# First attention of a two-layer perceiver: the folded sums of one pair and the turned row of maxima of another written as one step of VectorE's ring of PSUM banks

## The chip, the cores and the metric

The kernel runs on one core of one Trainium2 chip. The metric is the device time of one execution in microseconds; where a kernel is run several times, the median is given. A measurement of this kernel is repeatable to a few tenths of a per cent.

## What is computed

The reference is a stack of small layers over two sequences of 256 tokens of width 256 and two contexts of 4096 tokens of width 192. The change touches only its first layer, a cross-attention with 16 heads of width 16:

```
q = (x @ Wq + bq)    # (2, 256, 256)  -> 16 heads of 16
k = (ctx @ Wk + bk)  # (2, 4096, 256) -> 16 heads of 16
v = (ctx @ Wv + bv)
attn = softmax(einsum('bhqd,bhkd->bhqk', q, k) * 16 ** -0.5)   # 256 x 4096 for each head
x = x + (einsum('bhqk,bhkd->bqhd', attn, v).reshape(B, Nq, Cq) @ Wo + bo)
```

Everything behind it (a low-rank self-attention, an expert layer, a second cross-attention with a long convolution, a retention layer, adapters) is the same in both kernels.

## The kernel before, in words

**Pairs and steps.** The 32 (batch, head) combinations are taken two at a time: NP_ = 16 pairs, p = 0 to 15. Keys and queries lie in SBUF as stacks of 49 rows for each head of the pair, one head in partitions 0 to 48 and the other in partitions 64 to 112, so a matmul of the one and a matmul of the other stand side by side in the array. A pair has 16 steps, j = 0 to 15, each of 256 keys. In step j TensorE (`heads_tensor`) does, in this order:

- `scores(p, j)` (line 817, matmuls of line 827): keys by queries, transposed, 256 keys of both heads, four matmuls of 256 columns into one of three score banks (4 to 6) for each head. ScalarE takes their exponentials (`exps`, line 906), two ACTIVATEs of 128x512 for each step, into `pT`.
- `ahead(p, j)`: work for the next pair, five steps early (LEAD = 5). As a rule one `max_step` (line 766, matmuls of line 778): the plain scores of 128 queries and 512 keys of both heads, two matmuls of 512 columns. VectorE reduces them to row maxima (line 928, 128x1024 to 128x2). Sixteen such steps make the maxima of a pair.
- `weigh_half` (line 850, matmuls of line 839): the exponentials of earlier steps by V, four matmuls of 256 columns into four strips of 32 partitions of bank 7, recorded as eight since fp32 is done in two passes. The column of ones in V gives the sum of the softmax.

**The ring.** What TensorE makes for VectorE passes through a ring with two places of two banks each: place `at` uses banks 2*(at % 2) and 2*(at % 2)+1. The order of everything that passes is written out in the list `passing`, and `place[...]` gives the index. TensorE raises `max_made` when a place is filled and VectorE raises `max_read` when it has read it; before it fills place `at`, TensorE waits for the read of place `at - 2` (`max_read.at(at - 1)`). VectorE (`heads_vector`) works through `passing` in order. Three things pass besides the max steps:

- **rows** (`turn_rows`, lines 782 to 788; `add_rows`, lines 934 to 938). When the 16 maxima of pair p are there, VectorE reduces them once more to `nmax` (line 931). Two matmuls of 128 columns (line 787) turn them into a row, and VectorE adds that row to the queries `qs` (line 938). `ahead` issues this for pair p+1 in step j = 12 of pair p, right behind the second max step of pair p+2 and ahead of that step's weigh. `scores(p+1, 0)` waits for it.
- **sums** (`add_quarters`, lines 790 to 797; `take_sums`, lines 940 to 943). ScalarE copies bank 7 of pair p-1 to `oT` behind its fourth exponential of pair p (`sum_out`, line 912); `weigh` of pair p waits for that copy. In step j = 4 of pair p, behind the weigh, TensorE adds the four strips with the matrix `fold` (line 795: four matmuls of 128 columns into four strips of 32 partitions, recorded as eight) and VectorE copies the 128x128 result to `sums` (line 943). `sum_out` waits, before it writes `oT` again, until the fold that reads it is done.
- **turned** and the last sums, in pair 15 only: the stored sums are turned and divided by the sums of the softmax (`turn_sums`, `divide_turned`, `add_last`, `divide_last`).

So an ordinary pair fills 18 places: 16 max steps, one rows and one sums. In the steps of pair 14 from j = 11 on there is no next pair left, so no max steps are issued there, only the rows of pair 15.

Of the kernel before, what the change touches and what calls it, by code (L numbers as in the profile page):

```python
# [13 lines left out]
ALU = mybir.AluOpType  # L14
# [3 lines left out]
P = 128  # L18
# [4 lines left out]
S = 256  # L23
# [73 lines left out]
def build(nc, ins, out):  # L97
    pe, act, dve, pool, sp = nc.tensor, nc.scalar, nc.vector, nc.gpsimd, nc.sync
# [4 lines left out]
    def sb(name, shape, dt=F32):  # L103
        size = -(-math.prod(shape[1:]) * BYTES[dt] // 32) * 32
        spot[0] += size
        assert spot[0] <= END, (name, spot[0] - END)
        return nc.alloc_sbuf_tensor_at(name, shape, dt, offset=spot[0] - size)
# [28 lines left out]
    bank = nc.alloc_psum_tensor("bank", [P, 8, 512], F32)  # L136
# [166 lines left out]
    qs = [sb(f"qs{j}", [P, S], F32R) for j in range(3)]  # L303
# [223 lines left out]
    def keys_tensor():  # L527
# [84 lines left out]
    NP_ = NH // 2  # L612
# [11 lines left out]
    sums = sb("sums", [P, NP_ - 1, P])  # L624
    wo, bob = sb("wo", [P, 2, D]), sb("bob", [P, 1, D])
    oT = sb("oT", [P, 2 * S])
    fold = sb("fold", [P, 32])
# [8 lines left out]
    max_made, max_read, nmax_made = (flag(n) for n in ("max_made", "max_read", "nmax_made"))  # L636
    st_made, p_made, pv_made, oT_copied, den_made, o_done = (flag(n) for n in (
        "st_made", "p_made", "pv_made", "oT_copied", "den_made", "o_done"))
# [8 lines left out]
    def ahead(p, j):  # L647
        m, u = p + 1 + (j + LEAD) // 16, (j + LEAD) % 16
        return steps_of(m, u) if m < NP_ else [(NP_ - 1, "rows")] * (m == NP_ and u == 1)

    def beside(p, j):
        out = ahead(p, j) + [(p - 1, "sums")] * (j == 4 and p > 0)
        return out + [(j // TURN1, "turned")] * (p == NP_ - 1 and j in (TURN0, TURN1))

    passing = [what for u in range(16) for what in steps_of(0, u)]
# [5 lines left out]
    place = {what: at for at, what in enumerate(passing)}  # L661
# [103 lines left out]
    def heads_tensor():  # L765
# [16 lines left out]
        def turn_rows(p):  # L782
            at = place[p, "rows"]
            pe.wait_ge(*nmax_made.at(p + 1))
            pe.wait_ge(*max_read.at(at - 1))
            for qt in range(2):
                t = pe.matmul(bank[:, 2 * (at % 2), qt * P:(qt + 1) * P], nmax[:, qt, :], identr[:, :], start=True, stop=True)
            max_made.up(t)

        def add_quarters(p):  # L790
            at = place[p, "sums"]
            pe.wait_ge(*oT_copied.at(p + 1))
            pe.wait_ge(*max_read.at(at - 1))
            for c in range(4):
                t = pe.matmul(bank[32 * c:32 * c + 32, 2 * (at % 2), 0:P], fold[:, :], oT[:, c * P:(c + 1) * P],
                              start=True, stop=True)
            max_made.up(t)

        def add_last():
            at = place[NP_ - 1, "sums"]  # L800
# [78 lines left out]
        for p in range(NP_):  # L879
            for j in range(16):  # L880
                scores(p, j)
                for what in ahead(p, j):
                    pass_on(*what)
                weigh_half(16 * p + j)
                if j == 4 and p:
                    add_quarters(p - 1)
                if p == NP_ - 1:
                    if j in (TURN0, TURN1):
                        turn_sums(j // TURN1)
                    if j == 6:  # L890
                        turn_batch(0)
                    if j == 9:
                        project_batch(0)
# [6 lines left out]
    def heads_scalar():  # L900
        def exps(p, u):
            at = UNITS * p + u
            act.wait_ge(*st_made.at(at + 1))
            if at >= 8:
                act.wait_ge(*pv_made.at(2 * (at // 4 - 2) + 1 + at % 2))
            p_made.up(act.activation(pT[:, at % 8, :], bank[:, 4 + at % 3, :], ACT.Exp))  # L906

        def sum_out(p):
            act.wait_ge(*pv_made.at(16 * (p + 1)))
            if p:  # L910
                act.wait_ge(*max_made.at(place[p - 1, "sums"] + 1))
            oT_copied.up(act.copy(oT[:, :], bank[:, 7, :]))  # L912

        for p in range(NP_):
            for u in range(UNITS):
                exps(p, u)
                if u == 3 and p:
                    sum_out(p - 1)
        sum_out(NP_ - 1)
        act.wait_ge(*turned.at(4))  # L920
        xT_made.up(act.copy(xT[:, :, S:2 * S], bank[:, 1, :].rearrange("p (k n) -> p k n", k=2)))

    def heads_vector():
        def max_step(p, u):
            at, c, qt = place[p, u], u // 2, u % 2
            dve.wait_ge(*max_made.at(at + 1))
            b0 = 2 * (at % 2)
            max_read.up(dve.tensor_reduce(rmax[p % 2][:, :, qt, c], bank[:, b0:b0 + 2, :], AX.X, ALU.max))  # L928
            if u == 15:
                dve.wait_ge(*max_read.at(at + 1))  # L930
                nmax_made.up(dve.tensor_reduce(nmax[:, :, :].rearrange("p t (a m) -> p a t m", a=2)[:, :, :, MAX_ROW],
                                               rmax[p % 2][:, :, :, :], AX.X, ALU.max, negate=True))

        def add_rows(p):
            at = place[p, "rows"]
            rows = slice(0, HALF_P + MAX_ROW + 1)
            dve.wait_ge(*max_made.at(at + 1))
            max_read.up(dve.tensor_tensor(qs[p % 3][rows, :], bank[rows, 2 * (at % 2), 0:S], qs[p % 3][rows, :], ALU.add))

        def take_sums(p):  # L940
            at = place[p, "sums"]
            dve.wait_ge(*max_made.at(at + 1))
            max_read.up(dve.tensor_copy(sums[:, p, :], bank[:, 2 * (at % 2), 0:P]))

        def divide(total, p0, p1, read):
            den_made.up(dve.reciprocal(rden[:, p0:p1, :], total[:, :, :, D0]))
            dve.wait_ge(*den_made.at(den_made.n))
            for qt in range(2):
                t = dve.tensor_tensor(
                    aoc[:, 2 * (p0 // PB) + qt, :].rearrange("p (h a d) -> p h a d", h=PB, a=2)[:, p0 % PB:p0 % PB + p1 - p0],  # L950
                    total[:, :, qt:4:2, 0:D0],
                    rden[:, p0:p1, qt:4:2].rearrange("p h (a d) -> p h a d", d=1).to_broadcast([P, p1 - p0, 2, D0]), ALU.mult)
                if qt == 0:
                    aoc_made.up(t)
                else:
                    read.up(t)

        def divide_turned(b):
            at = place[b, "turned"]
            p0, p1 = b * PB, min((b + 1) * PB, NP_ - 1)  # L960
            if b == 0:
                dve.wait_ge(*powers_made.at(1))
            dve.wait_ge(*max_made.at(at + 1))
            total = bank[:, 2 * (at % 2):2 * (at % 2) + 2, :].rearrange("p b (n c k) -> p (b n) c k", n=4, c=4)
            divide(total[:, 0:p1 - p0], p0, p1, max_read)

        def divide_last():
            at = place[NP_ - 1, "sums"]
            dve.wait_ge(*max_made.at(at + 1))
            divide(bank[:, 2 * (at % 2), 0:P].rearrange("p (n c k) -> p n c k", n=1, c=4), NP_ - 1, NP_, max_read)  # L970

        def add_batch(b):
            if b == 0:
                dve.wait_ge(*turned.at(3))
                xT_made.up(dve.tensor_copy(xT[:, :, 0:S], bank[:, 1, :].rearrange("p (k n) -> p k n", k=2)))
                dve.wait_ge(*x_biased.at(1))
            dve.wait_ge(*proj_made.at(2 * b + 2))
            for i in (2 * b, 2 * b + 1):
                vec.do(dve.tensor_tensor(x[:, i, :], bank[:, 3, i % 2 * D:(i % 2 + 1) * D], x[:, i, :], ALU.add), x_added)

        nmax_zeroed.up(dve.memset(nmax[:, :, :].bitcast(F32), 0.0))
        fold_made.up(dve.tensor_copy(identr[:, :], ident[:, :]))
        pv_zeroed.up(dve.memset(bank[:, 7, :], 0.0))
        for q in range(4):
            fold_made.up(dve.tensor_copy(fold[32 * q:32 * q + 32, :], ident[0:32, 0:32]))
        dve.wait_ge(*nmax_zeroed.at(1))
        for p, u in passing:
            if u == "rows":
                add_rows(p)
            elif u == "turned":  # L990
                divide_turned(p)
            elif u == "sums" and p < NP_ - 1:
                take_sums(p)
                if p == NP_ - 2:
                    add_batch(0)
            elif u == "sums":
                divide_last()
            else:
                max_step(p, u)
        add_batch(1)  # L1000
# [1631 lines left out]
```

## Time and profile before

| | |
|---|---|
| median of 3 runs | 1071.77 us (1068.39 to 1072.86) |
| the profiled execution's own time | 1071.73 us |
| its span in the profile | 1070.5 us |
| PE busy | 927.4 us (87% of the span) |
| DVE busy | 815.2 us (76%) |
| ACT busy | 649.8 us (61%) |
| POOL busy | 303.5 us (28%) |

The span is what the profiler's instruction records cover; the execution's own time has 1.2 us more around it. PE is TensorE's matmuls, PEld its weight loads, DVE VectorE, ACT ScalarE, POOL GpSimd. The loop over the pairs, about 157 to 490 us of the span, is roughly a third of the kernel. In a timeline row the first number is the start in us from the span's beginning and the second the time from the first start to the last end of the merged instructions. The records of consecutive matmuls overlap, since their ends are modelled, so the distance between two starts says more than the length of a record.

### The profile page before, as it was taken

The page shows a single profiled execution, that of the slowest core. Times are in us where ns is not written, and L with a number is a line of the kernel's source. Part 1 is how long each engine was busy: PE and PEld are TensorE (multiplying, and loading weights), DVE is VectorE, ACT ScalarE, POOL GpSimd, SP SyncE. Part 2 cuts the span into 40 slices and gives each one's busy share as a digit, 9 for nine tenths or more (in the row PEclk, how much of TensorE's full clock was granted, in tenths as well). Part 3 has the DMA queues.
Part 4 walks back from the last instruction along what each step waited for, and adds up shares of the span by engine and source line. Part 5 has one row for each costly group of instructions (what it writes and reads, how often), then busy time and mean ns, then how long its engine had stood idle before and what let it go on. Part 6 is the DMA issues. An engine that isn't in the chain of part 4 may idle for free. (4 is left out here: it accounts for less than half of the span.)

```text
span 1070.5 us, 20952 instructions
## 1 busy us (share of the span) xinstructions
PE 927.4 (87%) x7731; PEld 578.0 (54%) x7731; DVE 815.2 (76%) x1703; ACT 649.8 (61%) x1045; POOL 303.5 (28%) x335
## 2 busy tenths in 40 slices
PE   6999669999999999998789996758788778899877
PEld 5989534444444444444466883733455556735545
DVE  5778599999999999961446887998877776269267
ACT  3434307888888888885245435159999999411212
POOL 1000088889800000000121632006454553000021
PEclk9999959999999999999699997666789999898979
DMA  6878933333323333300403308220165225771000
GB/s 203 296 271 281 321 83 76 80 81 77 85 74 84 79 78 83 79 17 1 121 1 103 90 16 219 83 64 1 57 167 149 60 57 156 221 184 59 0 1 20
DMA packets 99320, 111.83 MB, mean 104 GB/s; under 512 B 26658, under 2 KB 75730, under 8 KB 99218
## 3 DMA queue, kind: packets, MB, share of 16 engines
q1 hardware_dynamic: 98738, 110.16, 35.5%
q8 instruction: 62, 1.02, 0.4%
q10 hardware_dynamic: 480, 0.33, 0.1%
q14 instruction: 40, 0.33, 0.1%
HBM read 80.95 MB, written 29.43 MB: 103 GB/s over the span
## 5 line engine op out<-in xcount | busy, mean ns | idle before, releaser
L906 ACT ACTIVATE pT<-bank 128x512 f32<-128x512 f32 x512 | 278.4, 597 | 84.5 <-PE bank L827 66.9
L928 DVE TENSOR_REDUCE rmax<-bank 128x2 f32<-128x1024 f32 x256 | 309.9, 1224 | 19.4 <-PE bank L778 18.4
L839 PE MATMUL bank<-pT,V 128*17 128x256 f32 x2048 | 161.0, 386 | 4.0 <-ACT oT L912 3.9
L1823 PE MATMUL bank<-K1s,qs 97*128 97x512 f32 x256 | 113.3, 546 | 35.1 <-ACT work L1947 14.1
L827 PEld LDWEIGHTS bank<-qs,ks 49*128 49x128 f32 x1024 | 77.7, 186 | 108.2 <-ACT pT L906 97.6
L827 PE MATMUL bank<-qs,ks 49*128 49x256 f32 x1024 | 130.4, 332 | 2.1 <-ACT pT L906 0.5
L778 PE MATMUL bank<-ks,qs 49*128 49x512 f32 x512 | 112.0, 431 | 16.3 <-DVE rmax L928 7.4
L2112 POOL TENSOR_TENSOR total<-total,work 128x1024 f32<-128x1024 f32 x40 | 95.0, 2381 | 32.7 <-ACT work L1947 31.9
L1823 PEld LDWEIGHTS bank<-K1s,qs 97*128 97x128 f32 x256 | 53.4, 220 | 52.2 <-issue 36.1
L2007 DVE MAX8 cand<-work 128x8 f32<-128x128 f32 x384 | 76.4, 282 | 0.0
L839 PEld LDWEIGHTS bank<-pT,V 128*17 128x17 f32 x2048 | 34.4, 95 | 64.5 <-ACT pT L906 44.0
L778 PEld LDWEIGHTS bank<-ks,qs 49*128 49x128 f32 x512 | 51.0, 194 | 28.5 <-DVE rmax L928 15.6
L1857 PE MATMUL bank<-cn,xT 128*128 128x192 f32 x256 | 60.2, 388 | 6.8 <-ACT xT L1957 6.2
L1108 POOL MEMSET mA<- 128x512 f32 x1 | 0.5, 525 | 217.6 <-POOLq L115 217.6
L1857 PEld LDWEIGHTS bank<-cn,xT 128*128 128x128 f32 x256 | 50.7, 227 | 11.7 <-ACT xT L1957 10.4
L1947 ACT ACTIVATE work<-bank,ebias 128x1024 f32<-128x1024 f32 x48 | 53.8, 1127 | 4.5 <-PE bank L1826 4.2
L1826 PE MATMUL bank<-below,minus 128*128 128x512 bf16 x128 | 55.5, 434 | 0.0
L1938 ACT ACTIVATE below<-work,steep_thr,steep 128x2048 bf16<-128x2048 f32 (+1 forms) x26 | 51.7, 1989 | 2.3 <-issue 1.7
L1916 ACT COPY work<-bank 128x1024 f32<-128x1024 f32 x48 | 48.5, 1020 | 0.2 <-PE bank L1823 0.2
L1390 PE MATMUL bank<-xTp,w13p 128*128 128x512 f32 x192 | 47.2, 396 | 0.0
L1048 POOL TENSOR_TENSOR w13p<-w,w13p 128x512 fp32r<-128x512 f32 x16 | 20.5, 1284 | 74.7 <-ACT w13p L1042 74.7
L1390 PEld LDWEIGHTS bank<-xTp,w13p 128*128 128x128 f32 x192 | 35.1, 188 | 7.5
(470 smaller groups left out, 1782.5 us busy)
## 6 DMA issues: line engine op xcount, KB each, us to landing
k_parts_d<-kparts SPq DMA_DIRECT2D x48, 512.0 KB
ks<-k_parts_d SPq DMA_DIRECT2D x384, 64.0 KB, 2.2
K1s<-k_parts_d SPq DMA_DIRECT2D x96, 128.0 KB
cn<-in_ctx SPq DMA_DIRECT2D x32, 384.0 KB, 3.7
cx<-in_ctx SPq DMA_DIRECT2D x16, 384.0 KB, 4.6
w<-in_L_ffn_w SPq DMA_DIRECT2D x32, 128.0 KB, 2.4
w2e<-in_L_ffn_w SPq DMA_DIRECT2D x16, 128.0 KB, 2.4
W<-in_L_xattn_W SPq DMA_DIRECT2D x2, 1024.0 KB, 8.3
```

Of the source, the lines that this page charges most:

```text
L778: t = pe.matmul(bank[:, 2 * (at % 2) + a, :], qs[p % 3][rows, qt * P:(qt + 1) * P], ks[p % 2][rows, c * 512:(c + 1) * 512], start=True, st ...
L827: t = pe.matmul(bank[:, 4 + (at + a) % 3, c * S:(c + 1) * S], ks[p % 2][rows, k0:k0 + P], qs[p % 3][rows, :], start=True, stop=True)
L839: t = pe.matmul(bank[32 * c:32 * c + VW, 7, a * S:(a + 1) * S], V[:, b * NCH + 4 * g + c, h, :], pT[:, (at + 2 * (c // 2) + a) % 8, c % 2 ...
L906: p_made.up(act.activation(pT[:, at % 8, :], bank[:, 4 + at % 3, :], ACT.Exp))
L928: max_read.up(dve.tensor_reduce(rmax[p % 2][:, :, qt, c], bank[:, b0:b0 + 2, :], AX.X, ALU.max))
L1390: t = pe.matmul(bank[:, b0 + k, :], w13p[e % WB][:, wp, k, kt, :], xTp[:, xp, kt, :], start=(n == 0 and kt == 0), stop=(n == 2 and kt == 1))
L1823: m = pe.matmul(bank[:, b0 + c, :], qs1[0:NROW1, b * H1 + h, q], K1s[h][0:NROW1, keys], start=True, stop=(what == "new"))
L1826: m = pe.matmul(bank[:, b0 + c, :], minus[:, :], below[:, keys], start=False, stop=True)
L1857: m = pe.matmul(bank[:, 7, grp % 2 * 256:grp % 2 * 256 + DC], aT[at % 2][:, c, :], cn[at % NCN][:, c, :], start=(n == 0 and c == 0), stop= ...
L1947: s_taken.up(act.activation(home(t)[:, k * 1024:(k + 1) * 1024], bank[:, b0:b0 + 2, :].rearrange("p c n -> p (c n)"), ACT.Exp, bias=ebias[ ...
L2007: m = dve.max(cand[:, g, :], home(t)[:, g * GC:(g + 1) * GC])
L2112: added.up(pool.tensor_tensor(acc[:, part], acc[:, part], home(t)[:, part], ALU.add))
```

## The change

The sums of pairs 0 to 13 have no place of their own any more. The fold of pair p-2 is done in `turn_rows(p)` for p >= 2, behind the two matmuls of the rows, into the second bank of the same place, and `max_made` is raised once, behind the fold. In `add_rows(p)` VectorE adds the row and then copies the folded sums of pair p-2, and raises `max_read` once. In the order of TensorE the fold of pair p-1 moves from step j = 4 of pair p (behind the weigh) to step j = 12 of the same pair (between the rows and the weigh). An ordinary pair fills 17 places then. The sums of pair 14 keep their place in step j = 4 of pair 15, and those of pair 15 theirs at the end. ScalarE's wait in `sum_out` is set to the place that the fold has now.

```diff
     def beside(p, j):
-        out = ahead(p, j) + [(p - 1, "sums")] * (j == 4 and p > 0)
+        out = ahead(p, j) + [(p - 1, "sums")] * (j == 4 and p == NP_ - 1)
...
             for qt in range(2):
                 t = pe.matmul(bank[:, 2 * (at % 2), qt * P:(qt + 1) * P], nmax[:, qt, :], identr[:, :], start=True, stop=True)
+            if p >= 2:
+                pe.wait_ge(*oT_copied.at(p - 1))
+                t = fold_quarters(bank[:, 2 * (at % 2) + 1, 0:P])
             max_made.up(t)
+
+        def fold_quarters(o):
+            for c in range(4):
+                t = pe.matmul(o[32 * c:32 * c + 32, :], fold[:, :], oT[:, c * P:(c + 1) * P], start=True, stop=True)
+            return t
 
         def add_quarters(p):
             at = place[p, "sums"]
             pe.wait_ge(*oT_copied.at(p + 1))
             pe.wait_ge(*max_read.at(at - 1))
-            for c in range(4):
-                t = pe.matmul(bank[32 * c:32 * c + 32, 2 * (at % 2), 0:P], fold[:, :], oT[:, c * P:(c + 1) * P],
-                              start=True, stop=True)
-            max_made.up(t)
+            max_made.up(fold_quarters(bank[:, 2 * (at % 2), 0:P]))
...
-                if j == 4 and p:
+                if j == 4 and p == NP_ - 1:
                     add_quarters(p - 1)
...
             if p:
-                act.wait_ge(*max_made.at(place[p - 1, "sums"] + 1))
+                act.wait_ge(*max_made.at(place[(p + 1, "rows") if p < NP_ - 1 else (p - 1, "sums")] + 1))
             oT_copied.up(act.copy(oT[:, :], bank[:, 7, :]))
...
             dve.wait_ge(*max_made.at(at + 1))
-            max_read.up(dve.tensor_tensor(qs[p % 3][rows, :], bank[rows, 2 * (at % 2), 0:S], qs[p % 3][rows, :], ALU.add))
+            t = dve.tensor_tensor(qs[p % 3][rows, :], bank[rows, 2 * (at % 2), 0:S], qs[p % 3][rows, :], ALU.add)
+            if p >= 2:
+                t = dve.tensor_copy(sums[:, p - 2, :], bank[:, 2 * (at % 2) + 1, 0:P])
+            max_read.up(t)
```

## Rows read from the trace of the kernel before

**Rows 1.** The page: busy tenths in 40 slices of 26.8 us, and the clock.

```profile
PE   6999669999999999998789996758788778899877
...
DVE  5778599999999999961446887998877776269267
ACT  3434307888888888885245435159999999411212
...
PEclk9999959999999999999699997666789999898979
```

**Rows 2.** Windows: busy us (instructions) of PE, PEld, DVE, ACT, POOL; clock, DMA, GB/s.

```profile
160.00:168.00 8.00, 7.89 (x72) 3.43 (x72) 6.51 (x6) 5.61 (x12) 6.71 (x17) 0.74 0.20 51
...
184.00:480.00 296.00, 286.10 (x3253) 131.71 (x3252) 272.14 (x259) 247.06 (x461) 99.50 (x111) 1.00 0.29 75
```

**Rows 3.** Waits of 184 to 480 us: us in total, times, longest.

```profile
ACT pT L906 <- PE bank L827: 33.7, 97, 0.9
DVE rmax L928 <- PE bank L778: 15.1, 41, 0.4
...
PEld bank L778 <- DVE rmax L928: 4.5, 14, 0.3
```

**Rows 4.** Timeline of PE in pair 9, steps 3 to 6.

```profile
354.19 0.51 PE L827 MATMUL bank<-qs,ks 49*128 49x256 f32 x4
...
355.40 0.51 PE L827 MATMUL bank<-qs,ks 49*128 49x256 f32 x4
355.75 0.39 PE L778 MATMUL bank<-ks,qs 49*128 49x512 f32 x2
356.07 0.63 PE L839 MATMUL bank<-pT,V 128*17 128x256 f32 x8
356.51 0.40 PE L795 MATMUL bank<-oT,fold 128*32 128x128 f32 x8
356.85 0.51 PE L827 MATMUL bank<-qs,ks 49*128 49x256 f32 x4
357.46 0.50 PE L778 MATMUL bank<-ks,qs 49*128 49x512 f32 x2
357.89 0.63 PE L839 MATMUL bank<-pT,V 128*17 128x256 f32 x8
358.45 0.50 PE L827 MATMUL bank<-qs,ks 49*128 49x256 f32 x4
```

**Rows 5.** Timeline of DVE over the same steps.

```profile
354.96 2.45 DVE L928 TENSOR_REDUCE rmax<-bank 128x2 f32<-128x1024 f32 x2 [0.36 <-PE bank L778]
357.32 0.28 DVE L943 COPY sums<-bank 128x128 f32<-128x128 f32 x1
358.00 7.37 DVE L928 TENSOR_REDUCE rmax<-bank 128x2 f32<-128x1024 f32 x6 [0.40 <-PE bank L778]
```

**Rows 6.** Fold matmuls of line 795: durations ns min/median/max, first and last start.

```profile
L795 PE MATMUL bank<-oT,fold x120: 272/273/273, 186.1 to 483.9; 128*32 128x128 f32 x120
```

**Rows 7.** Timeline of PE in pair 0, steps 4 and 5, which have no sums.

```profile
164.30 0.50 PE L827 MATMUL bank<-qs,ks 49*128 49x256 f32 x4
...
165.52 0.50 PE L827 MATMUL bank<-qs,ks 49*128 49x256 f32 x4
```

**Rows 8.** Timeline of PE in pair 9, step 12, with the rows.

```profile
366.18 0.40 PE L778 MATMUL bank<-ks,qs 49*128 49x512 f32 x2
366.88 0.41 PE L787 MATMUL bank<-identr,nmax 128*128 128x128 f32 x2 [0.30 <-DVE rmax L928]
367.21 0.63 PE L839 MATMUL bank<-pT,V 128*17 128x256 f32 x8
367.77 0.51 PE L827 MATMUL bank<-qs,ks 49*128 49x256 f32 x4
368.11 0.41 PE L778 MATMUL bank<-ks,qs 49*128 49x512 f32 x2
```

**Rows 9.** Timeline of DVE over step 12 of pair 9.

```profile
367.78 0.41 DVE L938 TENSOR_TENSOR qs<-bank,qs 97x256 fp32r<-97x256 f32 x1
368.56 2.46 DVE L928 TENSOR_REDUCE rmax<-bank 128x2 f32<-128x1024 f32 x2 [0.36 <-PE bank L778]
```

**Rows 10.** Timeline of PE in pair 14, step 12, where no max steps are left.

```profile
472.76 0.44 PE L787 MATMUL bank<-identr,nmax 128*128 128x128 f32 x2
473.13 0.63 PE L839 MATMUL bank<-pT,V 128*17 128x256 f32 x8
473.69 0.51 PE L827 MATMUL bank<-qs,ks 49*128 49x256 f32 x4
```

## The prediction, made before the changed kernel was run

> **What bounds the kernel now.** The page's slices come first, to place the stage that is touched. From about slice 7 to slice 18 PE shows 9 tenths in each slice, DVE 9, ACT 8, and the clock stands at its upper level [rows 1]. This is the loop over the pairs, the only part that the edit reaches. The table of windows says the same of 184 to 480 us: PE 286.1 of 296 us, DVE 272.1, ACT 247.1, with a granted clock of 1.00, that is 2.4 GHz [rows 2]. Three engines lie within 15 per cent of each other, so shares don't decide; the timeline does.
>
> An ordinary step has one pace. In pair 0, which has no sums, steps 4 and 5 start 1.22 us apart (164.30 to 165.52) [rows 7]. VectorE takes six maxima in 7.37 us, 1.23 us for each [rows 5]. Its reduction and TensorE's own sequence (scores, max step, weigh) are equally long, so neither stores a lead over the other: an interruption of TensorE shows at once as an idle VectorE. The list of waits confirms it. TensorE waits for VectorE before a max step 14 times in the window, 4.5 us in all, once for each of the pairs 1 to 14, and VectorE's own idle time is 15.1 us in 41 waits, about three for each pair [rows 3]. So what costs time is the exceptional steps. There are three: the late copy of bank 7 (VectorE idle 0.36 us ahead of step 3's maximum), the sums (idle 0.40 us behind the copy of 0.28 us) [rows 5], and the rows (idle 0.36 us) [rows 9].
>
> **The price of a place for the sums.** In pair 9 the scores of steps 4, 5 and 6 start at 355.40, 356.85 and 358.45: 1.45 and 1.60 us, 3.05 together [rows 4]. Without sums two steps take 2.44 to 2.46. The first part is the fold itself. The second is the ring. VectorE reads the sums in 0.28 us, while the next max step can only be filled once the maximum before has been read: the reduction begun at 356.18 (half of the pair of 2.45 us begun at 354.96) ends at 357.41, and TensorE, ready some 0.35 us behind the scores of 356.85, starts at 357.46 [rows 4, 5]. A short place between two long ones leaves no time to refill. Without it the next max step goes into a place that has been free since 356.19, so the wait is gone and not moved: the scores start at about 356.63 (0.56 us behind the weigh of 356.07, as 357.89 to 358.45), the max step at 356.98, and VectorE goes on at 357.41, where it is done with the one before, instead of 358.00. That is 0.59 us earlier [rows 4, 5]. I take 0.60 us for each pair.
>
> It is removed from pairs 1 to 14. The fold's matmuls are 120 records of 8 each, 15 pairs, 186.1 to 483.9 us [rows 6]; the last of them, in pair 15, stays. So 14 times 0.60 = **8.4 us gained**.
>
> **The price of the fold in the rows' place.** Nothing is dropped: the same four matmuls (eight records of 273 ns that overlap [rows 6]) and the same copy are done in step 12. There TensorE sets the pace. It waits 0.30 us for the place, turns the row at 366.88, weighs at 367.21, scores at 367.77, fills the next place at 368.11, and VectorE starts on it at 368.56 after 0.36 us of idleness [rows 8, 9]. Whatever the fold takes on TensorE delays that chain in full. It can't slip into the wait of 0.30 us, since it stands behind the rows, which wait for the same place.
>
> How long is that? The trace doesn't show a fold between rows and weigh, so there are two bounds. Lower: inserting the fold between weigh and scores moved the scores from 0.56 us behind the weigh to 0.78 us (356.07 to 356.85), so 0.22 us. Upper: from the fold's start to the next start is 0.34 us (356.51 to 356.85) [rows 4]. I take 0.24, near the lower end, because what follows the fold now is a weigh, whose matmuls use strips of 32 columns as the fold's do, and weigh to fold was the quickest handover in these rows: 0.44 us, against 0.56 us from weigh to scores.
>
> The Trainium skill, page "TensorEngine Tiling (Array Packing)", section "Tiling Modes", says that a change of tiling mode drains TensorE. By it the move adds no such change: rows and weigh differ in mode already, and fold and weigh share one. The page would thus put the fold at the lower bound and the time at 1066.5 us, where the upper bound gives 1068.1; the trace agrees as far as the 0.44 against 0.56 us go [rows 4], and no row shows the handover from rows to fold.
>
> A lower end of zero is excluded, as TensorE has no slack in that stretch. 14 times 0.24 = **3.4 us lost** (3.1 to 4.8). In pair 14 step 12 has no max step and VectorE isn't pressed, but there too TensorE is late (0.93 us from rows to scores, 472.76 to 473.69, against 0.89 in pair 9, with no wait between [rows 8, 10]), so I count it in full.
>
> **VectorE's side of the same place.** The copy (0.28 us, some 0.2 of it beyond the end of the operation before [rows 5]) goes behind the add, which ends at 368.19. VectorE then idles until 368.56, later by the fold's 0.24: 0.6 us of cover for 0.28 [rows 9]. I cost it at nothing; without the cover it would be 0.28 us for each pair. The add needs the fold done now. TensorE would finish about 0.24 us behind 367.29, at 367.55 to 367.65, and VectorE is busy with the maximum before until about 367.78 [rows 8, 9]. That hides it too, with only 0.1 to 0.2 us to spare. Late next, if the fold took longer, would be the add and the copy, still within the idle time behind them.
>
> **The moved and changed waits.** TensorE's wait for `oT_copied` in step 12 is for a copy made around step 2 of the same pair, some 12 us earlier: nothing. ScalarE's wait in `sum_out` of the next pair is now for a fold five to six steps back instead of fourteen: nothing; ahead of it stand only exponentials. `scores(p+1, 0)` waits for the read of the rows' place, which ends 0.2 to 0.3 us later, with more than three steps (3.7 us) to spare. The other place of the ring is free by then, so the next max step doesn't wait; the one behind it needs the combined place at about 369.6, over 1 us after the copy. The ring's parity alternates from pair to pair, but 14 places fewer leave pair 15, with its fixed banks, as it was. No DMA is added, removed or passed: SP's and POOL's queues wait on flags of the scores, which only move with the loop.
>
> **The sum.** 8.4 gained less 3.4 lost is 5.0 us. The profiled execution took 1071.73 us, against a median of 1071.77, so I use the median: **1066.8 us**, 0.47 per cent less. By the bounds alone the gain lies between 3.5 and 5.4 us.
>
> **Rivals.**
>
> *The fold is absorbed* (faster than forecast). If TensorE catches up within the steps behind 12, because VectorE's 1.23 us and not TensorE's sequence is the true pace, a part of the 3.4 us comes back. VectorE would then have to find the 0.36 us idle before it elsewhere. For it: both paces agree to 0.01 us. Against it: VectorE's idle of 0.36 us behind the rows isn't recovered today, it simply passes. Time down to 1071.8 - 8.4 = 1063.4, on the way 1065. Chance 0.15.
>
> *The saving is small.* If the fold between two differently shaped neighbours costs 0.34 us, a restart behind it 0.11 (a weigh starts 0.43 us behind the max step that waited, 357.46 to 357.89, and 0.32 behind the one that didn't) and one more slow handover 0.12 (0.56 less 0.44) [rows 4], step 12 gives back 0.57. Then 14 times 0.03 is left, 1071.4. Against it: rows and weigh follow each other within 0.34 us today [rows 8]. Chance 0.15.
>
> *The stall moves along* (slower). The rows' place is longer now, and the next max step may meet it as the sums' neighbour did. Place: TensorE's first max steps behind step 12. Price: fold 0.34, copy 0.28 no longer covered, and the stall of the sums' place, 0.37 us (1.60 less 1.23 [rows 4]), together 0.99. It decides from 0.60 for each pair upward; at 0.99 the loss is 14 times 0.39 = 5.5 us, **1077.3**. Against it: a long place gives TensorE more time to refill, not less. Chance 0.05.
>
> *The change doesn't do what it says* could only be if the sums' stall came from the copy of bank 7. But the stall is at 357.46, and that copy's stands at step 3, in its own idle time [rows 4, 5]. I give it no chance of its own; it falls under the small saving.
>
> **How the numbers follow.** Forecast 0.65, absorbed 0.15, small saving 0.15, slower 0.05. Half a per cent, 5.4 us, is about what a measurement of this kernel can tell from no change, and the forecast lies just inside it. The runs before spread over 1068.39 to 1072.86, so the median itself may be off by 1 to 2 us, and of the forecast's 0.65 about 0.25 comes out faster by over 0.5 per cent. With the absorbed case: faster 0.40, same 0.55, slower 0.05. The range takes in the absorbed case and most of the small saving: 1063.0 to 1071.0.
>
> **What would show it.** In the profile after: scores of steps 4, 5 and 6 of pairs 1 to 14 at 1.22 to 1.23 us (right), or over 1.3 (wrong); no wait of a max step for a maximum in any of these pairs; the distance of step 12's scores to step 13's 2.16 to 2.28 us instead of 1.94 (366.18 less 0.35 to 367.77 [rows 8]); the weigh 0.56 to 0.67 us behind the rows instead of 0.34; copy of the sums straight behind the add, then idle time of 0.3 to 0.4 us. A distance of step 12 over 2.5 would make the forecast wrong, as would a new wait of the scores for the rows, or a stretch at the lower clock within the loop.

## The result and the profile after

The changed kernel takes 1065.32 us (median of 8 runs, 1061.87 to 1069.80), the kernel before 1072.12 (median of 8, 1068.39 to 1072.86). The ratio is 0.9943, with a 95% interval of 0.992 to 0.9965: 0.57 per cent faster, against a forecast of 1066.8 us, 0.47 per cent. The profiled execution of the changed kernel, 1061.87 us, is the fastest of its eight.

The page's head says what did not change: the work. DVE is busy for as long as before, to the tenth of a microsecond, with as many instructions.

```profile
span 1060.6 us, 20938 instructions
...
PE 919.9 (87%) x7731; PEld 573.3 (54%) x7731; DVE 815.2 (77%) x1703; ACT 650.1 (61%) x1045; POOL 303.6 (29%) x335
```

The table of windows shows where the time went. Each row is one stretch, with its length, the busy time of PE, PEld, DVE, ACT and POOL, the granted clock, the DMA share and GB/s. For each kernel the three rows are pair 0, pairs 1 to 14, and what lies behind the last scores of pair 15 (pair 15 itself, 21.4 us up to there in both, is left out). First the kernel before, then the changed one:

```profile
157.31:179.75 22.44, 21.85 (x213) 10.01 (x209) 20.55 (x20) 17.03 (x32) 18.89 (x45) 0.85 0.22 54
179.75:477.33 297.58, 287.47 (x3269) 132.22 (x3267) 276.34 (x262) 248.57 (x463) 103.02 (x120) 1.00 0.30 76
498.74:1070.49 571.75, 466.05 (x3286) 317.65 (x3286) 399.12 (x1216) 313.05 (x427) 155.25 (x106) 0.87 0.30 86
```

```profile
157.25:179.80 22.55, 21.95 (x212) 10.01 (x209) 20.56 (x20) 17.03 (x32) 18.95 (x45) 0.84 0.22 53
179.80:472.35 292.55, 283.91 (x3270) 130.52 (x3268) 276.29 (x262) 248.72 (x463) 103.19 (x120) 1.00 0.30 78
493.77:1060.63 566.86, 461.93 (x3286) 314.57 (x3286) 399.29 (x1216) 313.11 (x427) 155.09 (x106) 0.87 0.31 86
```

Pairs 1 to 14, the only ones that the edit reaches, take 292.55 us instead of 297.58: 5.03 us less, at a clock of 1.00 in both. The other 4.9 us of this pair of profiles lie behind the loop, in code that is the same. More on that below.

Within a pair, the PE timeline of pair 9 shows both terms of the sum. First the scores of steps 3 to 6, then step 12:

```profile
351.39 0.50 PE L832 MATMUL bank<-qs,ks 49*128 49x256 f32 x4
...
352.61 0.51 PE L832 MATMUL bank<-qs,ks 49*128 49x256 f32 x4
...
353.85 0.51 PE L832 MATMUL bank<-qs,ks 49*128 49x256 f32 x4
...
355.08 0.51 PE L832 MATMUL bank<-qs,ks 49*128 49x256 f32 x4
...
362.48 0.51 PE L832 MATMUL bank<-qs,ks 49*128 49x256 f32 x4
362.82 0.40 PE L778 MATMUL bank<-ks,qs 49*128 49x512 f32 x2
363.52 0.41 PE L787 MATMUL bank<-identr,nmax 128*128 128x128 f32 x2 [0.30 <-DVE rmax L933]
363.86 0.43 PE L795 MATMUL bank<-oT,fold 128*32 128x128 f32 x8
364.10 0.61 PE L844 MATMUL bank<-pT,V 128*17 128x256 f32 x8
364.65 0.50 PE L832 MATMUL bank<-qs,ks 49*128 49x256 f32 x4
364.98 0.40 PE L778 MATMUL bank<-ks,qs 49*128 49x512 f32 x2
```

Steps 4 and 5 start at 352.61, 353.85 and 355.08: 1.24 and 1.23 us, where it was 1.45 and 1.60 [rows 4]. The weigh of step 12 stands 0.58 us behind the rows (363.52 to 364.10) instead of 0.34 [rows 8], and step 12 is 2.17 us long (362.48 to 364.65). Over pairs 1 to 13 the mean of steps 4 and 5 together fell from 3.04 to 2.44 us and that of step 12 rose from 1.95 to 2.18. Summed over pairs 1 to 14, steps 4 and 5 gave 8.42 us, step 12 took 3.23, and the other thirteen steps together took 0.15 more, which makes the 5.0 us.

DVE's timeline answers to [rows 5, 9]:

```profile
352.17 9.85 DVE L933 TENSOR_REDUCE rmax<-bank 128x2 f32<-128x1024 f32 x8 [0.35 <-PE bank L778]
...
364.42 0.41 DVE L943 TENSOR_TENSOR qs<-bank,qs 97x256 fp32r<-97x256 f32 x1
364.75 0.28 DVE L945 COPY sums<-bank 128x128 f32<-128x128 f32 x1
365.42 7.39 DVE L933 TENSOR_REDUCE rmax<-bank 128x2 f32<-128x1024 f32 x6 [0.39 <-PE bank L778]
```

Eight maxima follow each other without a break where there were two, the copy, and a gap of 0.40 us. The copy now stands behind the add, and the gap behind it is 0.39 us, about what it was behind the add alone.

The waits of 184 to 480 us have no row any more for a max step that waits for VectorE, which had 14 entries [rows 3]. One wait changed its source: in pair 14, where no maxima are left, VectorE's add now waits 1.5 us for the fold, where it waited 1.1 us for the rows. VectorE's idle time ahead of a maximum is down by a third, from 15.1 us in 41 waits:

```profile
DVE rmax L933 <- PE bank L778: 10.0, 27, 0.4
```

### The profile page after: what moved, and what is told of

The parts are those of the page before. It is cut to its first block and busy times, and to the rows that moved or that the text cites. A ratio compares the mean times of both kernels' runs of the same rounds, so it can differ in the third digit from the quotient of the medians.

```text
span 1060.6 us, 20938 instructions
## 1 busy us (share of the span) xinstructions
PE 919.9 (87%) x7731; PEld 573.3 (54%) x7731; DVE 815.2 (77%) x1703; ACT 650.1 (61%) x1045; POOL 303.6 (29%) x335
## 5 line engine op out<-in xcount | busy, mean ns | idle before, releaser
L1865 PE MATMUL bank<-cn,xT 128*128 128x192 f32 x256 | 56.1, 369 | 6.4 <-ACT xT L1965 6.2
L1834 PE MATMUL bank<-below,minus 128*128 128x512 bf16 x128 | 57.7, 450 | 0.0
L1865 PEld LDWEIGHTS bank<-cn,xT 128*128 128x128 f32 x256 | 47.0, 213 | 11.2 <-ACT xT L1965 10.5
```

Of the source, the lines that this page charges most:

```text
L1834: m = pe.matmul(bank[:, b0 + c, :], minus[:, :], below[:, keys], start=False, stop=True)
L1865: m = pe.matmul(bank[:, 7, grp % 2 * 256:grp % 2 * 256 + DC], aT[at % 2][:, c, :], cn[at % NCN][:, c, :], start=(n == 0 and c == 0), stop= ...
```

## The experiments

Twelve runs followed: seven edited kernels, and five more profiles of the two kernels compared. The table gives, from the profile of each and of the first two, the stretches as above (us), the mean of steps 4 and 5 together and of step 12 over pairs 1 to 13, and the time at the lower clock behind the loop.

| kernel | pair 0 | pairs 1 to 14 | behind the loop | of it at the lower clock | steps 4 + 5 | step 12 |
|---|---|---|---|---|---|---|
| before | 22.4 | 297.58 | 571.8 | 154 | 3.04 | 1.95 |
| before_2 | 23.4 | 297.57 | 572.8 | 167 | 3.04 | 1.95 |
| before_3 | 23.3 | 297.46 | 573.0 | 154 | 3.04 | 1.95 |
| before_4 | 28.0 | 297.39 | 568.9 | 154 | 3.04 | 1.95 |
| changed | 22.6 | 292.55 | 566.9 | 143 | 2.44 | 2.18 |
| after_again | 23.3 | 292.79 | 567.2 | 150 | 2.45 | 2.18 |
| after_3 | 27.9 | 292.55 | 567.3 | 147 | 2.44 | 2.18 |
| no_sums | 27.0 | 289.39 | 568.8 | 150 | 2.44 | 1.95 |
| fold_twice_j4 | 22.4 | 297.41 | 568.0 | 147 | 3.05 | 1.95 |
| fold_twice | 26.1 | 295.52 | 571.7 | 154 | 2.44 | 2.40 |
| own_place | 26.0 | 302.62 | 568.1 | 147 | 2.44 | 2.97 |
| copy_twice | 23.3 | 292.51 | 567.7 | 137 | 2.44 | 2.18 |
| weigh_first | 23.3 | 289.89 | 570.3 | 160 | 2.44 | 1.95 |
| weigh_fold_rows | 27.8 | 288.42 | 567.7 | 143 | 2.45 | 1.82 |

Pairs 1 to 14 repeat within 0.3 us for one kernel, while over the profiles pair 0 moves by 5.6 us and the part behind the loop, whose code no edit touches, by 6.1. So the experiments are read by pairs 1 to 14.

**no_sums.** The gain without the cost.

```diff
-        out = ahead(p, j) + [(p - 1, "sums")] * (j == 4 and p > 0)
+        out = ahead(p, j) + [(p - 1, "sums")] * (j == 4 and p == NP_ - 1)
...
-                if j == 4 and p:
+                if j == 4 and p == NP_ - 1:
                     add_quarters(p - 1)
...
+        sums_filled.up(dve.memset(sums[:, :, :], 1.0))
```

> The kernel before, with the folds and copies of the sums of pairs 0 to 13 left out altogether (the stored sums are filled with ones once, so the attention's output is not the reference's). Theory of the ring: steps 4 and 5 of pairs 1 to 14 take 2.44 to 2.46 us together instead of 3.04, as in the changed kernel, and step 12 takes 1.95 as before. The loop is 8.4 us shorter than before and 3.2 to 3.4 us shorter than in the changed kernel. Rival (what the changed kernel gained in steps 4 and 5 is only its fold's own time on TensorE, 0.22 to 0.34 us for each pair, and the rest comes from somewhere else): steps 4 and 5 at 2.7 to 2.8.

Measured: 8.2 us less than before in pairs 1 to 14 (8.4 in steps 4 and 5, 0.2 back in the other steps), and 3.2 less than the changed kernel. Steps 4 and 5 take 2.44 us. The gain of steps 4 and 5 is the whole place, as the theory has it, and what the changed kernel gives back in step 12 is the rest.

**fold_twice_j4.** Is it the fold's own time, or the place?

```diff
-            for c in range(4):
+            for c in (*range(4), *range(4)):
                 t = pe.matmul(bank[32 * c:32 * c + 32, 2 * (at % 2), 0:P], fold[:, :], oT[:, c * P:(c + 1) * P],
```

> The kernel before, with every fold of step 4 done twice, one behind the other into the same strips. Theory of the ring: TensorE waits for the maximum before in step 5 anyway, 0.27 us behind the point at which it would be ready, and a second fold takes about 0.22 us. So the scores of step 5 come 0.22 us later, the wait shrinks by as much, and steps 4 and 5 together stay at 3.04 to 3.10; the loop grows by 0 to 0.8 us. Rival (the fold's time on TensorE is what the place costs): steps 4 and 5 at 3.26 to 3.38, the loop 3 to 5 us longer.

Its PE timeline, steps 4 and 5 of pair 9:

```profile
354.52 0.51 PE L827 MATMUL bank<-qs,ks 49*128 49x256 f32 x4
...
355.64 0.62 PE L795 MATMUL bank<-oT,fold 128*32 128x128 f32 x16
356.19 0.50 PE L827 MATMUL bank<-qs,ks 49*128 49x256 f32 x4
356.59 0.50 PE L778 MATMUL bank<-ks,qs 49*128 49x512 f32 x2
...
357.58 0.51 PE L827 MATMUL bank<-qs,ks 49*128 49x256 f32 x4
```

Sixteen records where there were eight. Step 4 grows to 1.67 us (354.52 to 356.19) and step 5 shrinks to 1.39 (to 357.58), 3.06 together as before (3.05). Pairs 1 to 14 take 297.41 us, not a tenth more. In step 4 the fold costs nothing: without it TensorE would only stand still for as long, until VectorE has read the maximum before and so the place of the next max step. The rows of before show what is left as the price: that maximum ends at 357.41, the max step starts at 357.46 and VectorE goes on at 358.00 [rows 4, 5]. These 0.59 us pass whatever the fold takes, as long as it fits into the wait, and the copy lies inside them.

**fold_twice.** The same doubling in the changed kernel.

```diff
-                t = fold_quarters(bank[:, 2 * (at % 2) + 1, 0:P])
+                for _ in range(2):
+                    t = fold_quarters(bank[:, 2 * (at % 2) + 1, 0:P])
```

> The changed kernel, with the fold in the rows' place done twice. Theory (TensorE sets the pace in step 12, so the fold is paid in full there): step 12 goes from 2.18 to 2.40 to 2.42 us, the loop grows by 14 times 0.22, 3.1 us. Rival (VectorE sets the pace, or the fold slips into its idle time): step 12 stays within 0.05 us of 2.18, the loop within 0.7 us.

Its PE timeline, in step 12 of pair 9, which runs from 366.82 to 369.21:

```profile
368.21 0.64 PE L796 MATMUL bank<-oT,fold 128*32 128x128 f32 x16
368.67 0.61 PE L845 MATMUL bank<-pT,V 128*17 128x256 f32 x8
369.21 0.50 PE L833 MATMUL bank<-qs,ks 49*128 49x256 f32 x4
```

The weigh starts 0.46 us behind the doubled fold, where it was 0.24. Measured: step 12 at 2.40 us in the mean, pairs 1 to 14 longer by 2.97 us, 0.21 for each. The fold is free in step 4 and paid in full in step 12.

**own_place.** The move without the sharing.

```diff
-        out = ahead(p, j) + [(p - 1, "sums")] * (j == 4 and p > 0)
+        out = ahead(p, j) + [(p - 1, "sums")] * (j == (4 if p == NP_ - 1 else 12) and p > 0)
...
                 for what in ahead(p, j):
                     pass_on(*what)
+                if j == 12 and 0 < p < NP_ - 1:
+                    add_quarters(p - 1)
                 weigh_half(16 * p + j)
-                if j == 4 and p:
+                if j == 4 and p == NP_ - 1:
                     add_quarters(p - 1)
```

> The kernel before, with the sums moved to step 12, right behind the rows and ahead of the weigh, but still in a place of the ring of their own. It has the changed kernel's order of matmuls, without the shared place. Theory of the ring: the fold must wait there until the maximum before the rows has been read, about 0.75 us more than in the changed kernel, and the weigh, the scores and the next max step stand behind it. Step 12 takes 2.9 to 3.1 us, steps 4 and 5 take 2.45; the loop is 9 to 12 us longer than in the changed kernel, that is 4 to 7 us longer than before. Rival (it is the move to step 12 that helps, not the sharing): step 12 at 2.2 to 2.4, the loop within 3 us of the changed kernel.

Its PE timeline in step 12:

```profile
371.84 0.41 PE L787 MATMUL bank<-identr,nmax 128*128 128x128 f32 x2 [0.30 <-DVE rmax L930]
372.97 0.42 PE L795 MATMUL bank<-oT,fold 128*32 128x128 f32 x8 [0.72 <-DVE rmax L930]
373.19 0.64 PE L839 MATMUL bank<-pT,V 128*17 128x256 f32 x8
```

The fold waits 0.72 us for the maximum before the rows. Step 12 takes 2.97 us; pairs 1 to 14 take 302.62 us, 10.1 more than in the changed kernel and 5.0 more than before. Moving alone loses as much as moving and sharing gains.

**copy_twice.** Is VectorE's copy covered?

```diff
-                t = dve.tensor_copy(sums[:, p - 2, :], bank[:, 2 * (at % 2) + 1, 0:P])
+                for k in (p - 1, p - 2):
+                    t = dve.tensor_copy(sums[:, k, :], bank[:, 2 * (at % 2) + 1, 0:P])
```

> The changed kernel, with the copy of the sums in the rows' place done twice (the first into the slot of the next pair, which is overwritten later). Theory (the copy stands in VectorE's idle time behind the add, 0.39 us): a second one takes 0.20 to 0.28 us of it; the idle time falls to 0.1 to 0.2 us, step 12 stays at 2.18 and the loop within 0.5 us. Rival (VectorE sets the pace there): step 12 at 2.38 to 2.46, the loop 2.8 to 3.9 us longer.

Its DVE timeline:

```profile
363.82 0.42 DVE L943 TENSOR_TENSOR qs<-bank,qs 97x256 fp32r<-97x256 f32 x1
364.15 0.48 DVE L946 COPY sums<-bank 128x128 f32<-128x128 f32 x2
364.82 2.46 DVE L933 TENSOR_REDUCE rmax<-bank 128x2 f32<-128x1024 f32 x2 [0.19 <-PE bank L778]
```

The second copy adds 0.20 us, the idle time falls from 0.39 to 0.19, and pairs 1 to 14 stay at 292.51 us. The copy is covered, and the idle time left behind it is almost twice what it adds.

**weigh_first and weigh_fold_rows.** Can the wait of 0.30 us ahead of the rows be filled, and does the order of shapes matter? The first issues the weigh of step 12 ahead of the rows:

```diff
                 for what in ahead(p, j):
-                    pass_on(*what)
+                    if what[1] != "rows":
+                        pass_on(*what)
                 weigh_half(16 * p + j)
+                for what in ahead(p, j):
+                    if what[1] == "rows":
+                        pass_on(*what)
```

> The changed kernel, with the weigh of step 12 issued ahead of the rows and the fold instead of behind them. Theory (TensorE waits 0.30 us for the rows' place and has the weigh to fill that with): the weigh runs during that wait, the rows start at nearly the same point, and the scores of step 13 come 0.3 us earlier. Step 12 takes 1.85 to 1.90 us instead of 2.18, 15 times 0.3 = 4.5 us less than the changed kernel in the loop. Rival (the chain through VectorE, maximum, add, copy, sets step 12): step 12 stays above 2.1 us. Ratio to before 0.988 to 0.993 by the theory, 0.992 to 0.998 by the rival.

The second puts the fold ahead of the two matmuls of the rows as well:

```diff
+            if p >= 2:
+                pe.wait_ge(*oT_copied.at(p - 1))
+                fold_quarters(bank[:, 2 * (at % 2) + 1, 0:P])
             for qt in range(2):
                 t = pe.matmul(bank[:, 2 * (at % 2), qt * P:(qt + 1) * P], nmax[:, qt, :], identr[:, :], start=True, stop=True)
-            if p >= 2:
-                pe.wait_ge(*oT_copied.at(p - 1))
-                t = fold_quarters(bank[:, 2 * (at % 2) + 1, 0:P])
```

> As weigh_first, and the fold ahead of the rows, so that weigh and fold, which both use strips of 32 columns, stand together. Theory: one handover between differently shaped matmuls less, 0.1 us; TensorE could reach step 13 0.4 us earlier than in the changed kernel, and there VectorE (maximum, add, copy without a break) becomes the bound of that stretch at about 0.39. Step 12 takes 1.76 to 1.82 us in pairs 1 to 13, the loop is 5.5 to 6 us shorter than the changed kernel's. Rival (the order of shapes makes no difference): step 12 as in weigh_first within 0.02.

The PE timeline of step 12, weigh_first:

```profile
361.17 0.40 PE L778 MATMUL bank<-ks,qs 49*128 49x512 f32 x2
361.50 0.63 PE L844 MATMUL bank<-pT,V 128*17 128x256 f32 x8
362.05 0.44 PE L787 MATMUL bank<-identr,nmax 128*128 128x128 f32 x2
362.42 0.42 PE L795 MATMUL bank<-oT,fold 128*32 128x128 f32 x8
362.78 0.51 PE L832 MATMUL bank<-qs,ks 49*128 49x256 f32 x4
```

And weigh_fold_rows (line 790 is the rows):

```profile
364.93 0.40 PE L778 MATMUL bank<-ks,qs 49*128 49x512 f32 x2
365.26 0.63 PE L844 MATMUL bank<-pT,V 128*17 128x256 f32 x8
365.70 0.40 PE L795 MATMUL bank<-oT,fold 128*32 128x128 f32 x8
366.04 0.44 PE L790 MATMUL bank<-identr,nmax 128*128 128x128 f32 x2
366.40 0.51 PE L832 MATMUL bank<-qs,ks 49*128 49x256 f32 x4
```

The wait is gone in both. weigh_first gives 2.66 us in pairs 1 to 14, less than the 4.5 of its expectation (which counted pair 0 too): step 12 is 1.95 us, not 1.85 to 1.90. The expectation had the rows start at nearly the same point, but they start 0.88 us behind the max step (361.17 to 362.05) instead of 0.70 (362.82 to 363.52): from weigh to rows are 0.55 us (361.50 to 362.05), against 0.44 from weigh to fold (365.26 to 365.70), and rows to fold and fold to scores, 0.37 and 0.36, are no shorter. In pair 14, where there is no wait to fill, step 12 even grew, from 1.59 to 1.71 us. With the fold beside the weigh step 12 falls to 1.82 us, at the upper end of its expectation, and to 1.57 in pair 14. The 4.13 us less in pairs 1 to 14 stay under the 5.5 to 6 expected of the loop, since step 12 gained 0.36 us in pairs 1 to 13 rather than 0.39, step 13 gave back 0.04 (the next max step comes 0.34 us behind its scores, 366.40 to 366.74, but VectorE's rows show no wait from the add at 366.53 to the maximum at 367.21, so VectorE sets the pace there), and step 12 of pair 14, with no VectorE to wait for, gained only 0.01 to 0.02.

In repeated runs weigh_fold_rows took 1059.35 us (median of 5, 1056.94 to 1063.10), a ratio to before of 0.987 (0.9849 to 0.9891); weigh_first 1063.56 us (median of 6), 0.9912 (0.9882 to 0.9942). Weigh_fold_rows is faster than both the kernel before and the changed one (1065.86 in the same comparison).

**after_again, before_2, before_3, before_4, after_3.** No edit: more profiles of the two kernels, to see whether the 4.9 us behind the loop belong to the change.

> The changed kernel once more. The first comparison gave 6.8 us less, the profiles of the two 5.0 us less in pairs 1 to 14 and 4.9 us less behind the loop. Theory (only pairs 1 to 14 changed; what else differs is the chance of how long the clock stays at its lower level in pair 0 and behind the loop): pairs 1 to 14 again at 292.5 us, and the part behind the loop anywhere between 566 and 572 us, longer where more of it is spent at the lower clock. Rival (the part behind the loop is shorter in the changed kernel for good): again below 567.5 us. Ratio to before over the rounds: 0.992 to 0.998 by both.

> The kernel before, unchanged, for another profile. Theory (the part behind the loop and pair 0 differ by chance, with the time spent at the lower clock): pairs 1 to 14 again at 297.5 us within 0.3; the part behind the loop between 566 and 572 us, and not the 571.8 of the first profile by necessity; pair 0 near 22.4 or, with a later rise of the clock, up to 28 us. Rival (the kernel before is slower behind the loop for good): 571 to 572 us again.

> As before_2: a third profile of the kernel before. Theory: pairs 1 to 14 at 297.5 us, the part behind the loop between 566 and 572 us. Rival: 571 to 572 us.

> A third profile of the changed kernel. Theory: pairs 1 to 14 at 292.5 us, the part behind the loop between 566 and 572 us. Rival (it is shorter there for good): below 567.5 us, as in its first two profiles.

> A fourth profile of the kernel before. Behind the loop the three so far took 571.8, 572.8 and 573.0 us, the three of the changed kernel 566.9, 567.2 and 567.3, with the same code there; six experiments lay between 567.7 and 571.7. Theory (chance): with even odds 570 us or less. Rival (the kernel before is slower behind the loop by its own timing): 571.5 to 573 us again. Pairs 1 to 14 at 297.5 us by both.

After_again gave 1065.86 us (median of 8), a ratio of 0.9946 (0.9923 to 0.997) to a median of 1072.90. Its 567.2 us behind the loop, and then 572.8, 573.0 and 567.3, fell as the rival wanted: three of before at 571.8 or more, three of the changed kernel at 567.3 or less. The fourth profile of before did not. Its windows, in the same order as above:

```profile
156.24:184.21 27.97, 27.37 (x212) 11.93 (x209) 20.58 (x20) 17.03 (x32) 23.46 (x57) 0.65 0.15 43
184.21:481.60 297.39, 287.09 (x3270) 132.30 (x3268) 276.18 (x262) 248.69 (x463) 98.71 (x109) 1.00 0.28 76
503.02:1071.87 568.85, 464.20 (x3272) 317.46 (x3286) 399.06 (x1216) 313.14 (x427) 155.24 (x106) 0.86 0.31 86
```

568.9 us behind the loop, with no edit, and 28.0 us in pair 0 at a mean clock of 0.65, where the first profile had 22.4 at 0.85. And the experiments, which have the same code behind the loop too, lie between 567.7 (copy_twice, weigh_fold_rows) and 571.7 (fold_twice), with fold_twice_j4, whose loop is as long as before's, at 568.0. (There were seven of them, not six as the last expectation says.) So one kernel moves by 4 us there and by 5.6 us in pair 0, and neither follows the edit without exception. Two things keep this from being a proof of chance. The profiles come from several chips: before_2, before_3 and after_3 from one, where the two of before gave 572.8 and 573.0 and the changed kernel 567.3, and before_4 from another. And all four profiles of before still lie above all three of the changed kernel. That the kernel before is always at 571.5 us or more there is refuted; that it is slower there on the average is neither shown nor excluded, and the cause, be it the chip, the clock or the shift of 5 us in time, stays open.

## Why the prediction was right

**What bounds the loop**: right. TensorE's and VectorE's paces are equal, and only the exceptional steps cost.

**The price of the sums' place**, 0.60 us for each pair, 8.4 in all: measured 0.60 and 8.42 in steps 4 and 5 of the changed kernel, and 8.2 us net over the whole pairs by no_sums. Its splitting was wrong in one point. "The first part is the fold itself. The second is the ring" holds for where the time is seen, not for what costs it. The fold's 0.22 us in step 4 are free, as fold_twice_j4 showed; the ring takes the whole 0.60.

**The price of the fold in the rows' place**, 0.24 us: measured 0.23 (2.18 less 1.95), 3.2 us in 14 pairs, where the forecast had 3.4. The choice near the lower bound was right, and the timeline shows why: from the fold to the weigh behind it are 0.24 us (363.86 to 364.10), from a fold to scores 0.34 [rows 4] and 0.36 (weigh_first). The Trainium skill's rule in "TensorEngine Tiling (Array Packing)", section "Tiling Modes", that a change of mode drains the engine, agrees with these handovers: by the distances between starts, the change of shape adds 0.10 to 0.12 us here. No run shows whether a drain is what takes this time. Pair 14 paid in full, as forecast: step 12 from 1.36 to 1.59 us.

**VectorE's side**: right, with the numbers. Of the 0.6 us of cover the copy took 0.2 and left 0.39, and the fold ended 0.13 us before VectorE wanted the place (363.86 and 0.43, against the add at 364.42).

**The moved waits**: all cost nothing. The one whose source changed, VectorE's add in pair 14, grew by 0.4 us with nothing behind it: the scores of pair 15, which wait for that place, start at 472.35, 3.3 us behind the end of the copy (468.74 and 0.28).

**The sum**: forecast 5.0 us, measured 5.03 in pairs 1 to 14, and 4.6 to 5.0 over the other profiles. That it fits to 0.03 is in part luck: the fold took 0.2 us less than forecast, and the other steps gave 0.15 back, which the sum had at nothing. The range of the gain by the bounds alone is 3.6 to 5.3 us (8.4 less 4.8 and 3.1), not 3.5 to 5.4. The comparisons gave 6.8 and 7.0 us with intervals of 3.8 to 8.6 and 3.2 to 8.3 (one less the ratio's bounds, times the median), which hold the 5.0. The 1.8 to 2.0 us beyond are not explained by any step of the prediction, so that the total fell within the range with more in it than the mechanism that was forecast. Over all timed runs the means are 1072.2 (21 runs) and 1065.9 us (16 runs), 6.3 apart with a standard error of 0.8. That leaves 1.3 us, less than two of these errors, which may be chance or an effect behind the loop that these runs can't tell from it. It stays open.

**The rivals**: the absorbed fold falls by fold_twice, the small saving by the 2.18 us of step 12, the stall that moves along by the missing waits. Own_place shows where the last would have been true: in a place of its own, the fold meets just such a stall.

## What to carry to other kernels

In a ring with two places, a short item between two long ones costs the time in which the producer can't refill, whatever its own work, as long as that fits into the wait; here 0.6 us for a copy of 0.28. Pack it into a place that is short anyway and behind which the consumer is idle already. Then look at which matmuls it stands beside: beside the weigh, which uses the same strips, instead of between the rows and the scores, it made step 12 0.14 us shorter (1.82 against 1.95 us, and 1.57 against 1.71 in pair 14). Where a wait of the producer remains, put independent work of it in front: together with that order it gave another 4.1 us here.

## What was not expected of the hardware

The lower clock (1.2 GHz) after TensorE's idle stretch ahead of the loop (no matmul from 127 to 130 us in the first profile) lasted until 163 to 166 us in eight of the fourteen profiles and until 171 to 176 in six, with the same code up to there but for one memset in no_sums. Pair 0 takes 22.4 to 23.4 us in the first case and 26.0 to 28.0 in the second. What decides between them no run shows. Behind the loop the time at the lower clock was 137 to 167 us, and it goes with the length of that part only loosely: 154 us of it stood in profiles of 568.9 and of 573.0. Executions of the kernel before, one program, lay between 1068.39 and 1076.43 us, 8 us apart and more than the change itself, while pairs 1 to 14, at a granted clock of 1.00 throughout, repeat to 0.1 per cent. For a change of half a per cent, the stretch that it touches tells more than the total.
